# Two attention stages of a four-layer kernel: scores in row groups, a reordered step, and the residual moved to Pool

## The chip, the cores and the metric

One program runs on one core of a Trainium2 chip. The metric is the device time of one execution in microseconds; the kernel before took 2830.82 us (median of 3 runs, 2821.55 to 2833.54).

## The reference

Four layers act on x of shape 16 items x 256 tokens x 128 features. Each layer is: normalise, scale and shift (the "modulation"), attention, gated residual; then normalise, modulate, feed-forward, gated residual. The change touches the attention of layers 0 and 1 only.

```python
# layer 0 attention: 16 heads of 64
q = (x @ Wq).reshape(B, N, H, Dh)            # scale 64**-0.5
k, v = halves of x @ Wkv
s = einsum('bhid,bhjd->bhij', q * scale, k)
gm = max(s, axis=-1)                         # before masking
p = where(causal_mask, 0, exp(s - gm))
out = (p @ v) / (sum(p) + EPS)
return out.reshape(B, N, H * Dh) @ Wo + bo
# layer 1 attention: 8 heads of 128, plus scores of relative position, softmax, then @ w_out + b_out
# after either:  x = x + gate * attention(modulated(norm(x)))
```

## The kernel before, in words

Items are processed one after another. `walk` issues the same list of steps on each engine (PE, ACT, DVE, Pool, SP); an item has PER = 8 steps, there are 128 steps in a stage, and a loop body holds two items. Engines are coupled by semaphores only, so on each engine the order written in `step` is the order of execution. In a step `at`, `nx` (or `n1`, `n2`) are steps ahead whose projections are made, and `b1`, `b2`, `b3` are steps behind whose softmax, P^T and values are finished.

**Layer 0 (`attention0`, L393 to L633).** One step is one pair of heads. A = Wq Wk^T per head (64 rows deep, L496) is made once before the loop, for 16 heads, and split in a rounded and a rest part in fp32r. A product of two such split operands is `matmul3` (L120): three matmuls, recorded as L122, L123, L124. PE issues in a step: transposes of P for b2 (L383, six); scores of `at` as xA x hT, two heads one after the other, each 2 row blocks x 3 matmuls of 256 columns, 128 rows deep (L122 to L124, `xA` in the rows); projections xA for nx (two `matmul3`, with `A` in the rows) and between them V for nx in fp32 (L533); four small bf16 matmuls that add the causal mask (L540, L542), two for each head after its row maximum; P^T V for b2 in two column groups of 64 (L552); the output projection for b3 (L563). ACT copies o (L465), the second head's P^T (L469), rounds xA (L480, twice), copies V (L482) and makes the exponentials (L457, L459: two of each in a step). DVE copies the first head's P^T (L597), takes the row maxima (L602, one for each head), adds EPS, takes the reciprocal and scales P (L610, L612, L617), and writes the rest of xA (L625, twice). The residual of an item is on DVE: bias and gate at the end of the step with p = 2 (L183, L188), add and row statistics in the step p = 3 (L191, L195). Once per item, in step p = 5, PE transposes the normalised rows of the item after next (L507) into the free half of the bank of the first xA; ACT modulates and rounds them (L389, L131), Pool makes the rest (L138).

**Layer 1 (`attention1`, L925 to L1285).** One step is one head. PE: transposes of P (L1140), projection (A in the rows), scores (xA), in half of the steps the values (VO), six matmuls for the position scores (a_R), P^T V accumulated over the heads in one of two banks `y_ps` (L1190). SP writes the position scores to DRAM and reads them back shifted. ACT: P^T (L1051), xA (L1056), values (L1062), exponentials (L1074). DVE: L1246, L1249, L1253, the sum with the shifted scores and its maximum (L1265), L1270, position scores (L1276), and the residual as in layer 0. The item's transposes (L1179) go in step p = 3 into the free half of the bank `qh_ps` of the projection, so they wait for DVE's L1253, and the projection of step p = 4 waits for ACT's modulation (L389), which ACT does before the exponentials of that step.

Weights are loaded by DMA into an arena; in layer 0 the DVE waits for the gate's DMA before its loop.

Of the kernel before, what the change touches and what calls it, by code (L numbers as in the profile page):

```python
# [94 lines left out]
class Norms:  # L95


    def __init__(self, nc, ctx):
# [12 lines left out]
        self.delta = sb("delta", [P, NT, P])  # L111
        self.hT = sb("hT", [P, 2, T])
# [86 lines left out]
def residual_by_pool(pool, n, at, y, gate, y_ready, each, weighted, added, item=False):  # L199
# [4 lines left out]
    pool.tensor_tensor(n.delta[:], y, g, ALU.mult).then_inc(weighted, 1)  # L204
    wait(pool, weighted, at, item=True)
# [151 lines left out]
class Shared:  # L357
# [8 lines left out]
    [("wqT0", (16, P), 64), ("wkT0", (16, P), 64), ("wv0", (1024,), P), ("wo0", (8, P), P), ("bo0", (P,), P)],  # L366
# [26 lines left out]
def attention0(nc, d, k):  # L393
# [7 lines left out]
    with ExitStack() as ctx:  # L401
        def sb(name, shape):
            return ctx.enter_context(nc.sbuf_tensor("a0_" + name, shape, F32))

        A = ctx.enter_context(nc.sbuf_tensor("a0_A", [P, 2 * PER, 2, P], F32R))
        xA = ctx.enter_context(nc.sbuf_tensor("a0_xA", [P, 4, 2, T], F32R))
        v = sb("v", [P, 4, NT, P])
# [7 lines left out]
        xA_ps = k.banks[0:2]  # L415
        s_ps, pT_ps = k.banks[2:4], k.banks[4:6]
        o_ps, y_ps = k.banks[6], k.banks[7]
        names = ("chain", "var", "std", "rstd", "xn", "ht_mm", "ht", "ht_rounded", "ht_cut", "A_mm", "A_rounded", "A_cut",
                 "xA_mm", "xA_rounded", "xA", "v", "s_mm",
                 "nmax", "masked", "exp", "den", "rec", "p", "pT_mm", "pT0", "pT1", "o_mm", "oT", "y_mm", "res")  # L420
        s = signals(nc, ctx, "a0_", names)
        LAST, LEAD, LAG = PER - 1, 6, 4

        def halves(x, i, first, end):
            return [x[:, i, part, first:end] for part in range(2)]

        with nc.Block() as block:
# [5 lines left out]
            @block.gpsimd  # L433
            def _(pool):
                def step(at):
                    ni = at.shift(3)
                    if at.p == 5 and ni.real:
                        cut_hT_rest(pool, n, ni, s["ht_rounded"], s["ht_cut"])

                walk(pool, PER, 2, LEAD, LAG, step)  # L440

            @block.scalar
            def _(act):
                std_of_rows(act, n, s["var"], s["std"])
                for h in range(2 * PER):
                    act.wait_ge(s["A_mm"], h + 1)
                    act.activation(A[:, h, 0, :], k.banks[h % 4][:, 0:P], ACT.Identity, scale=64 ** -0.5
                                   ).then_inc(s["A_rounded"], 1)

                def step(at):  # L450
# [10 lines left out]

                    if b3.real:
# [7 lines left out]
                    if at.p == 5:  # L470
                        ni = at.shift(3)
                        if ni.real:
                            wait(act, s["ht_mm"], ni, item=True)
                            modulated(act, k, phase, ni, xA_ps[0][:, T:2 * T], n.hT[:, ni.s // PER % 2, :], s["ht"])
                            cut_hT(act, n, ni, s["ht"], s["ht_rounded"])
                    if nx.real:
                        wait(act, s["s_mm"], nx.shift(-2), 2)
                        for h in range(2):
                            wait(act, s["xA_mm"], nx, 2, 1 - h)
                            act.copy(xA[:, 2 * nx.ring(2) + h, 0, :], xA_ps[h][:, 0:T]).then_inc(s["xA_rounded"], 1)  # L480
                        wait(act, s["o_mm"], nx.shift(-4))
                        act.copy(v[:, nx.ring(4)], xA_ps[1][:, T:2 * T].rearrange("p (t d) -> p t d", t=NT)).then_inc(s["v"], 1)  # L482
# [8 lines left out]
            def _(pe):  # L491
                pe.wait_ge(k.weights_in[phase], 16 * weight_pieces(phase))
                for h in range(2 * PER):
                    if h >= 4:
                        pe.wait_ge(s["A_cut"], h - 3)
                    pe.matmul(k.banks[h % 4][:, 0:P], w["wqT0"][:, h, :], w["wkT0"][:, h, :], start=True, stop=True  # L496
                              ).then_inc(s["A_mm"], 1)
                pe.wait_ge(s["A_cut"], 2 * PER)

                def step(at):  # L500
                    nx, b1, b2, b3 = at.shift(1), at.shift(-1), at.shift(-2), at.shift(-3)
                    ni = at.shift(3)
                    if at.p == 5 and ni.real:
                        wait(pe, s["xn"], ni, item=True)
                        wait(pe, s["xA"], at, 2, 1)
                        for t in range(NT):
                            mm = pe.transpose(xA_ps[0][:, T + t * P:T + (t + 1) * P], n.xn[:, t, :], k.ident[:])  # L507
# [7 lines left out]
                    if at.real:  # L515
                        for h in range(2):
                            wait(pe, s["xA"], at, 2, 1 - h)
# [1983 lines left out]
```

## Time and profile before

| | |
|---|---|
| median of 3 runs | 2830.82 us |
| the profiled execution's own time | 2832.67 us |
| its span (first to last instruction) | 2831.0 us |
| busy PE, PEld, DVE, ACT, POOL over the span | 2580.4, 2224.2, 1999.8, 1420.3, 590.2 us |
| layer 0 attention, loop | about 46 to 697 us |
| layer 1 attention, loop | about 1020 to 1545 us |

PE is the tensor engine's matmuls, PEld its weight loads, which run beside them. A matmul's recorded duration holds its latency; what it costs in a stream is the distance from its start to the next one's. "x6" in a row of the timeline means six instructions of that kind in a row, told by the start of the first and the time to the end of the last.

### The profile page before, as it was taken

To read this page: it belongs to the slowest core of one execution; us is meant where nothing else is said; L and a number is where in the kernel's file an instruction comes from. 1 tells how busy PE (TensorE), PEld (TensorE's weight loads), DVE (VectorE), ACT (ScalarE), POOL (GpSimd) and SP (SyncE) were. 2 spreads that over 40 slices of the span, in tenths; PEclk is the share of its full clock that TensorE was granted. 3 is DMA by queue.
4 is the path that set the end of the run, shared out by engine and by line. 5 is a ranking of instruction groups with operands and counts; after the bars stand their busy time and mean duration, and the time that the engine had idled before them with its cause. 6 is when DMAs were issued, how large, how long until landed. Compare 5 with 4: busy or idle time off the path is not lost. (4 is left out here: it accounts for less than half of the span.)

```text
span 2831.0 us, 65632 instructions
## 1 busy us (share of the span) xinstructions
PE 2580.4 (91%) x21002; PEld 2224.2 (79%) x21064; DVE 1999.8 (71%) x6254; ACT 1420.3 (50%) x4003; POOL 590.2 (21%) x1099
## 2 busy tenths in 40 slices
PE   5999999998999999999997999968998886999898
PEld 5988888887888879999996999955665464666566
DVE  4888888887677658888887677756775325677687
ACT  3666666666555445566665322314555222455544
POOL 0000000000111100000000111136775025777322
PEclk9999999999999999999999999979999897999899
DMA  5000000001100145555554000037553753655100
GB/s 146 2 2 1 1 1 1 1 1 35 30 0 0 47 131 159 159 166 167 167 166 135 9 0 0 0 86 206 153 144 98 85 60 102 163 152 147 41 14 17
DMA packets 196040, 212.11 MB, mean 75 GB/s; under 512 B 12628, under 2 KB 179940, under 8 KB 194420
## 3 DMA queue, kind: packets, MB, share of 16 engines
q1 hardware_dynamic: 195828, 209.64, 27.8%
q8 instruction: 89, 1.46, 0.2%
q14 instruction: 123, 1.01, 0.1%
HBM read 108.95 MB, written 90.65 MB: 71 GB/s over the span
## 5 line engine op out<-in xcount | busy, mean ns | idle before, releaser
L138 POOL TENSOR_TENSOR hT<-hT 128x256 fp32r<-128x256 f32 x64 | 47.0, 735 | 1415.6 <-ACT hT L131 1415.6
L122 PE MATMUL bank<-hT,a_xA 128*128 128x256 f32 x768 | 228.0, 297 | 10.4 <-DVE a_top L1265 7.6
L123 PE MATMUL bank<-hT,a_xA 128*128 128x256 f32 x768 | 216.8, 282 | 0.0
L124 PE MATMUL bank<-hT,a_xA 128*128 128x256 f32 x768 | 216.3, 282 | 0.0
L602 DVE TENSOR_REDUCE a_nmax<-bank 128x2 f32<-128x512 f32 x256 | 175.0, 690 | 56.6 <-PE bank L124 54.3
L1074 ACT ACTIVATE a_p<-a_p,a_nmax 128x256 f32<-128x256 f32 x256 | 128.3, 502 | 163.5 <-DVE a_nmax L1270 163.5
L1723 ACT ACTIVATE a_p<-bank 128x1024 f32<-128x1024 f32 (+1 forms) x256 | 193.4, 808 | 24.2 <-PE bank L1778 20.0
L480 ACT CAST a_xA<-bank 128x256 fp32r<-128x256 f32 x256 | 95.0, 373 | 198.2 <-PE bank L124 198.2
L1351 ACT ACTIVATE f_silu<-bank 128x512 f32<-128x512 f32 x128 | 76.5, 598 | 214.9 <-PE bank L124 214.9
L799 ACT ACTIVATE f_hidden<-bank,arena 128x256 f32<-128x256 f32 x256 | 120.5, 473 | 114.9 <-PE bank L124 113.7
L862 PE MATMUL bank<-arena,f_hidden 128*128 128x128 f32 x1024 | 172.0, 288 | 6.4 <-DVE f_acc L916 5.0
L1666 POOL TENSOR_SCALAR_AFFINE_SELECT a_p<-a_p 128x512 f32<-128x512 f32 x256 | 163.8, 640 | 0.0
L916 DVE SCALAR_TENSOR_TENSOR f_acc<-bank,f_cw,f_acc 128x128 f32<-128x128 f32 x448 | 134.8, 345 | 40.0 <-PE bank L862 37.0
L1932 DVE TENSOR_REDUCE a_nmax<-bank 128x4 f32<-128x1024 f32 x128 | 155.6, 1216 | 3.9 <-PE bank L1765 3.9
L122 PE MATMUL bank<-hT,f_w 128*128 128x256 f32 x512 | 156.0, 305 | 0.3 <-POOL hT L138 0.3
L122 PEld LDWEIGHTS bank<-hT,a_xA 128*128 128x128 f32 x768 | 145.2, 189 | 13.0 <-issue 12.5
L862 PEld LDWEIGHTS bank<-arena,f_hidden 128*128 128x128 f32 x1024 | 137.0, 192 | 19.3 <-DVE f_acc L916 11.1
L123 PEld LDWEIGHTS bank<-hT,a_xA 128*128 128x128 f32 x768 | 145.5, 189 | 0.0
L123 PE MATMUL bank<-hT,f_w 128*128 128x256 f32 x512 | 145.5, 284 | 0.0
L124 PE MATMUL bank<-hT,f_w 128*128 128x256 f32 x512 | 145.4, 284 | 0.0
L124 PEld LDWEIGHTS bank<-hT,a_xA 128*128 128x128 f32 x768 | 145.2, 189 | 0.0
L1190 PE MATMUL bank<-a_v,a_pT 128*128 128x128 f32 x1024 | 136.3, 276 | 4.9 <-ACT a_pT L1051 4.9
(309 smaller groups left out, 8144.1 us busy)
## 6 DMA issues: line engine op xcount, KB each, us to landing
pos_dram<-a_pos SPq DMA_DIRECT2D x128, 383.0 KB
a_stack<-rows_dram SPq DMA_DIRECT2D x128, 320.0 KB, 4.1
rows_dram<-a_cut SPq DMA_DIRECT2D x192, 192.0 KB, 2.4
a_shifted<-pos_dram SPq DMA_DIRECT2D x128, 256.0 KB, 2.7
f_merged<-f_staged SPq DMA_DIRECT2D x16, 578.0 KB, 9.0
gate<-gates_dram SPq DMA_DIRECT2D x32, 256.0 KB, 10.8
arena<-in_task SPq DMA_DIRECT2D x4, 1156.0 KB, 8.4
x<-in_x SPq DMA_DIRECT2D x4, 512.0 KB, 8.3
```

Of the source, the lines that this page charges most:

```text
L122: pe.matmul(out, left[0], right[0], start=start, stop=False, skip_group_check=True)
L123: pe.matmul(out, left[0], right[1], start=False, stop=False, skip_group_check=True)
L124: return pe.matmul(out, left[1], right[0], start=False, stop=stop, skip_group_check=True)
L602: dve.tensor_reduce(nmax[:, at.ring(2), h, :], s_ps[h][:].rearrange("p (t k) -> p t k", t=NT), AX_X, ALU.max, negate=True).then_inc(s["nma ...
L799: act.activation(hidden[:, nx.ring(2), :], h_ps[nx.ring(2)][:, 0:T], ACT.Relu, bias=w["e1b"][:, nx.p:nx.p + 1]).then_inc(s["hidden"], 1)
L862: mm = pe.matmul(y, hidden[:, at.ring(2), t * P:(t + 1) * P], w["e2w"][:, at.p, :], start=(t == 0), stop=not last, skip_group_check=True)
L916: i = dve.scalar_tensor_tensor(out=a, in0=z, scalar=c[:, t, at.p:at.p + 1], in1=a, op0=ALU.mult, op1=ALU.add)
L1074: i = act.activation(p[:, at.ring(4), t, :], p[:, at.ring(4), t, :], ACT.Exp, bias=nmax[:, r, t:t + 1], accum_out=sums[:, r, t:t + 1])
L1190: mm = pe.matmul(y[:, t * P:(t + 1) * P], pT[:, b2.ring(2), j, t * P:(t + 1) * P], v[:, slot, j, h * P:(h + 1) * P], start=(b2.p == 0 and ...
L1666: pool.affine_select(blocks, blocks, [[0, 4], [1, P]], ALU.is_ge, 0.0, base=0, channel_multiplier=-1).then_inc(s["causal"], 1)
L1723: act.activation(p[:, b4.ring(2), first:end], sT_ps[:, first:end], ACT.Exp).then_inc(s["exp"], 1)
L1932: dve.tensor_reduce(nmax[:, half, 1, of], s_ps[:, 2 * T:6 * T].rearrange("p (c q) -> p c q", c=4), AX_X, ALU.max, negate=True).then_inc(s[ ...
```

## The change

In layer 0, A is no longer made: q and k are projected for both heads of a pair at once (`qk`, 128 rows = 2 heads x 64), and the scores are q^T k with 64 rows depth, head 0 on rows 0 to 63 of the array, head 1 on rows 64 to 127, issued alternately into two banks. V is projected in split fp32r, 256 columns wide (two head pairs) for one block of tokens per step. Both heads' scores signal once at their end. The mask of head 1 is issued after P^T V. In both layers the residual's bias, gate and add go to Pool, after ACT has copied the sum from PSUM (`take_sum`), and DVE keeps the statistics, one step later in layer 0. In layer 1 the item's transposes go into the free `y_ps` bank, and ACT does them after the exponentials. The copy of the first head's P^T by DVE is the same line before and after.

```diff
@@ helpers
+def take_sum(act, n, at, y, y_ready, biased, taken):
+    wait(act, y_ready, at)
+    wait(act, biased, at.shift(-at.per), item=True)
+    act.copy(n.y[:], y[:, 0:T].rearrange("p (t d) -> p t d", t=NT)).then_inc(taken, 1)
+
+def biased_residual_by_pool(pool, n, at, gate, bias, taken, biased, weighted, added):
+    wait(pool, added, at.shift(-at.per), item=True)
+    wait(pool, taken, at, item=True)
+    pool.tensor_tensor(n.delta[:], n.y[:], bias, ALU.add).then_inc(biased, 1)
+    wait(pool, biased, at, item=True)
+    g = gate[:, at.item, :].unsqueeze(1).to_broadcast([P, NT, P])
+    pool.tensor_tensor(n.delta[:], n.delta[:], g, ALU.mult).then_inc(weighted, 1)
+    wait(pool, weighted, at, item=True)
+    pool.tensor_tensor(n.x[:, at.item, :, :], n.x[:, at.item, :, :], n.delta[:], ALU.add).then_inc(added, 1)
@@ attention0, before the loop
-                for h in range(2 * PER):
-                    pe.matmul(k.banks[h % 4][:, 0:P], w["wqT0"][:, h, :], w["wkT0"][:, h, :], ...)
+                for i in range(6):        # ACT rounds, DVE makes the rest, 128x512 each
+                    act.activation(W[:, x, 0, part], whole, ACT.Identity, scale=scale).then_inc(s["W_rounded"], 1)
+                pool.wait_ge(k.gate_in[phase], 16 * GATE_PIECES)     # and no longer DVE
@@ attention0, PE
-                        for h in range(2):
-                            wait(pe, s["xA"], at, 2, 1 - h)
-                            wait(pe, s["exp"], at.shift(-1), 2, 1 - h)
-                            for t in range(NT):
-                                mm = matmul3(pe, s_ps[h][:, t * T:(t + 1) * T],
-                                             halves(xA, 2 * at.ring(2) + h, t * P, (t + 1) * P),
-                                             halves(n.hT2, at.s // PER % 2, 0, T), start=(t == 0))
-                            mm.then_inc(s["s_mm"], 1)
+                        wait(pe, s["qk"], at, 2)
+                        wait(pe, s["exp"], at.shift(-1), 2)
+                        for t in range(NT):
+                            for a, c in ((0, 0), (0, 1), (1, 0)):
+                                for h in range(2):
+                                    mm = pe.matmul(s_ps[h][:, t * T:(t + 1) * T],
+                                                   qk[64 * h:64 * h + 64, at.ring(2), 0, a, t * P:(t + 1) * P],
+                                                   qk[64 * h:64 * h + 64, at.ring(2), 1, c, :], ...)
+                        mm.then_inc(s["s_mm"], 1)
...
-                            for t in range(NT if h else 0):
-                                pe.matmul(xA_ps[1][:, T + t * P:T + (t + 1) * P], n.hT[:, item, t * P:(t + 1) * P],
-                                          w["wv0"][:, c:c + P], start=True, stop=True)
-                            matmul3(pe, xA_ps[h][:, 0:T], halves(A, 2 * nx.p + h, 0, P), halves(n.hT2, item, 0, T)
+                            if i:
+                                matmul3(pe, qk_ps[1][:, T:2 * T], halves(n.hT2, item, t * P, (t + 1) * P),
+                                        [W[:, 2, part, first:first + 2 * P] for part in range(2)])
+                            matmul3(pe, qk_ps[i][:, 0:T], [W[:, i, part, nx.p * P:(nx.p + 1) * P] ...
...
+                    if at.real:
+                        mask(0)
                     if b2.real:
                         ...               # P^T V
+                    if at.real:
+                        mask(1)
@@ attention1, PE
-                        if at.p == 4:
-                            wait(pe, s["ht"], at.shift(4), item=True)
...
-                        wait(pe, s["xA"], n2)
-                            mm = pe.transpose(qh_ps[:, T + t * P:T + (t + 1) * P], n.xn[:, t, :], k.ident[:])
+                        wait(pe, s["taken"], ni.shift(-2 * PER), item=True)
+                            mm = pe.transpose(y_ps[ni.s // PER % 2][:, t * P:(t + 1) * P], n.xn[:, t, :], k.ident[:])
```

## Rows read from the trace of the kernel before

**Rows 1.** The page, part 1: busy us, share and instructions of each engine.

```profile
PE 2580.4 (91%) x21002; PEld 2224.2 (79%) x21064; DVE 1999.8 (71%) x6254; ACT 1420.3 (50%) x4003; POOL 590.2 (21%) x1099
```

**Rows 2.** Busy time by window: PE, PEld, DVE, ACT, POOL (count), then clock, DMA.

```profile
50.00:690.00 640.00, 633.03 (x5603) 567.65 (x5602) 519.60 (x1502) 436.10 (x1686) 11.00 (x15) 1.00 0.01 2
1020.00:1545.00 525.00, 501.11 (x3675) 482.26 (x3673) 428.54 (x1643) 306.23 (x863) 11.11 (x15) 0.99 0.51 160
```

**Rows 3.** Source view of L480: count, min/median/max ns, first and last start.

```profile
L480 ACT CAST a_xA<-bank x256: 372/373/378, 47.3 to 684.6; 128x256 fp32r<-128x256 f32 x128
```

**Rows 4.** Timeline of PE, one step of layer 0: start, us, instruction, count.

```profile
300.84 0.37 PE L122 MATMUL bank<-hT,a_xA 128*128 128x256 f32 x1
...
302.35 0.28 PE L122 MATMUL bank<-hT,a_A 128*128 128x256 f32 x1
...
302.70 0.61 PE L533 MATMUL bank<-arena,hT 128*128 128x128 f32 x4
303.06 0.36 PE L122 MATMUL bank<-hT,a_A 128*128 128x256 f32 x1
...
303.51 0.23 PE L540 MATMUL bank<-causal_bf,ident_bf 128*128 128x128 bf16 x1
...
303.69 0.22 PE L542 MATMUL bank<-causal_bf,ident_bf 128*128 128x128 bf16 x1
303.83 0.87 PE L552 MATMUL bank<-a_pT,a_v 128*64 128x256 f32 x8
304.64 0.71 PE L563 MATMUL bank<-arena,a_oT 128*128 128x128 f32 x4
305.18 0.82 PE L383 MATMUL bank<-ident,a_p 128*128 128x128 f32 x6
305.76 0.36 PE L122 MATMUL bank<-hT,a_xA 128*128 128x256 f32 x1
...
311.02 0.36 PE L122 MATMUL bank<-hT,a_xA 128*128 128x256 f32 x1
```

**Rows 5.** Timeline of PE in windows of 70 and 90 ns inside L552.

```profile
303.83 0.44 PE L552 MATMUL bank<-a_pT,a_v 128*64 128x256 f32 x2
...
304.43 0.28 PE L552 MATMUL bank<-a_pT,a_v 128*64 128x128 f32 x2
```

**Rows 6.** Timeline of ACT, same step.

```profile
303.70 0.37 ACT L480 CAST a_xA<-bank 128x256 fp32r<-128x256 f32 x1 [0.43 <-PE bank L124]
...
305.74 0.23 ACT L459 ACTIVATION_READ_ACCUMULATOR a_p<-bank,a_nmax 128x1 f32 x1
```

**Rows 7.** Timeline of DVE, same step.

```profile
301.83 1.41 DVE L602 TENSOR_REDUCE a_nmax<-bank 128x2 f32<-128x512 f32 x2 [0.48 <-PE bank L124]
...
304.49 0.75 DVE L625 TENSOR_TENSOR a_xA<-bank,a_xA 128x256 fp32r<-128x256 f32 x2
```

**Rows 8.** Timeline of all engines, first item of layer 0.

```profile
42.92 0.60 DVE L171 TENSOR_SCALAR xn<-x,row_mean,row_rstd 128x128 f32<-128x128 f32 x2 [3.29 <-DMA gate<-gates_dram]
...
45.45 0.72 POOL L138 TENSOR_TENSOR hT<-hT 128x256 fp32r<-128x256 f32 x1 [44.93 <-ACT hT L131]
...
46.23 0.58 PE L122 MATMUL bank<-hT,a_A 128*128 128x256 f32 x1 [1.90 <-POOL hT L138]
```

**Rows 9.** Timeline of DVE, end of layer 0.

```profile
696.99 0.42 DVE L183 TENSOR_TENSOR delta<-bank,arena 128x256 f32<-128x256 f32 x1 [2.43 <-PE bank L563]
...
698.37 0.49 DVE L195 BATCH_NORM_STATS2 row_stats<-x 128x6 f32<-128x128 f32 x2
```

**Rows 10.** Source view of L206, Pool's add in other stages.

```profile
L206 POOL TENSOR_TENSOR x<-x,delta x64: 722/732/995, 731.6 to 2826.8; 128x256 f32<-128x256 f32 x32, 128x256 f32 x32
```

**Rows 11.** Timeline of layer 1, PE around the item's transposes.

```profile
1299.02 0.34 PE L124 MATMUL bank<-a_R,hT 128*128 128x384 f32 x1
1299.95 0.44 PE L1179 MATMUL bank<-ident,xn 128*128 128x128 f32 x2 [0.59 <-DVE a_xA L1253]
```

**Rows 12.** Waits in 1050 to 1540 us: us in total, times, longest.

```profile
PE bank L1179 <- DVE a_xA L1253: 10.0, 14, 1.3
```

More of the change, by code:

```diff
@@ L492, in _ @@
                 pe.wait_ge(k.weights_in[phase], 16 * weight_pieces(phase))
[L493 to L498, printed above, removed]
+                pe.wait_ge(s["W_cut"], 6)
                 def step(at):
@@ L556, in step @@
                         mm.then_inc(s["o_mm"], 1)
+                    if at.real:
+                        mask(1)
                     if b3.real:
                         wait(pe, s["oT"], b3)
-                        before = b3.shift(-PER)
-                        if b3.p == 0 and before.real:
-                            pe.wait_ge(s["chain"], before.item * 3 + 3)
+                        if b3.p == 0:
+                            wait(pe, s["taken"], b3.shift(-PER), item=True)
                         for t in range(NT):
@@ L604, in step @@
                                               negate=True).then_inc(s["nmax"], 1)
-                    if after:
-                        residual(at.shift(-4), "stats").then_inc(s["res"], 1)
+                    if at.p == 4 and at.shift(-5).real:
+                        row_stats(dve, n, at.shift(-5), s["added"])
                     if b1.real:
@@ L1184, in step @@
                         y, slot, h = y_ps[b2.s // PER % 2], b2.s // 4 % 2, b2.p % 4
-                        before = b2.shift(-2 * PER)
-                        if b2.p == 0 and before.real:
-                            pe.wait_ge(s["chain"], before.item * 3 + 3)
+                        if b2.p == 0:
+                            wait(pe, s["ht"], b2, item=True)
                         for t in range(NT):
@@ L1226, in _ @@
                 dve.wait_ge(s["r_in"], 16)
-                dve.wait_ge(k.gate_in[phase], 16 * GATE_PIECES)
-                def residual(item, *parts):
-                    y = y_ps[item.s // PER % 2]
-                    return add_residual(dve, n, item, y[:, 0:T].rearrange("p (t d) -> p t d", t=NT),
-                                        k.gate[phase % 2], w["bo1"].unsqueeze(1).to_broadcast([P, NT, P]), s["chain"],
-                                        3, parts)
                 def step(at):
                     n2, b1, b3 = at.shift(2), at.shift(-1), at.shift(-3)
-                    ended = b3.real and b3.p == LAST
-                    after = at.shift(-4).real and at.p == 3
-                    if after:
-                        residual(at.shift(-4), "add")
                     if at.p == 1 and at.shift(7).real:
@@ L1255, in step @@
                                                  op0=ALU.add, op1=ALU.subtract).then_inc(s["xA"], 1)
-                    if after:
-                        residual(at.shift(-4), "stats").then_inc(s["res"], 1)
+                    if at.p == 3 and at.shift(-4).real:
+                        row_stats(dve, n, at.shift(-4), s["added"])
                     if at.real:
@@ L1278, in step @@
                         i.then_inc(s["pos"], 1)
-                    if ended:
-                        wait(dve, s["y_mm"], b3)
-                        residual(b3, "bias")
-                    if ended:
-                        residual(b3, "gate")
                 walk(dve, PER, 2, LEAD, LAG, step)
```

142 lines of the change are left out of this document (76 added, 66 removed).

## The prediction

> **What bounds the kernel now.** Start with the page: PE is busy for 91% of the span, but that is a mean over eight stages [rows 1]. The windows give the two stages that are edited: in layer 0's loop PE is busy 633 of 640 us, DVE 520, ACT 436; in layer 1's loop PE 501 of 525 and DVE 429 [rows 2]. Both are PE's. The source view gives layer 0's step: 256 roundings are 128 steps, the first at 47.3 and the last at 684.6, about 0.8 us of which lies inside a step, so 636.5 / 127 = 5.01 us each, 40.1 us an item [rows 3]. The timeline shows a plain step, from the first score at 300.84 to the next at 305.76: 4.92 us without a hole, and then one of 5.26 [rows 4]. Matmuls of 256 columns start 0.118 us apart: three go from 302.35 to 302.70.
>
> The parts of the plain step, start to start [rows 4]: 12 scores 1.42 (1.51 as recorded, the first takes over 0.09 from the transposes); the two projections 0.71; V 0.44 (0.36 and the 0.09 of late start that follows); masks 0.23; a gap of 0.09; P^T V from 303.83 to 304.64, 0.81; output projection 0.54; six transposes 0.66. Sum 4.90.
>
> **Layer 0, PE.** Whether scores of 64 rows run in pairs no row shows. The nearest is P^T V, in two column groups: both starts of a pair fall in one window of 70 ns, twice [rows 5]. Its eight records take 0.81 us; four fp32 records of 128 columns alone need 0.11 each, and four of 256 at least twice that, 1.3 us one after another. So column groups run in pairs, their weight loads too. I take the same for row groups: 6 pairs x 0.118 = 0.71 instead of 1.42. The other end is no overlap at all, 12 x 0.118 = 1.42. I choose the first, since the partner of each matmul is in another bank and other rows, as it is in other columns there.
>
> A change of shape is not free in the same rows: between the end of the last mask (303.69 + 0.06) and L552 are 0.09 us, and L552's last records start at 304.43 and stream 0.11, but L563 begins at 304.64, another 0.09, and its first weights are then loaded with nothing beside them, 0.11 [rows 4, 5]. So scores cost 0.71 + 0.09 + 0.11 = 0.91 and the projections behind them 0.20 more.
>
> The Trainium skill (TensorEngine Tiling (Array Packing), Key Properties) says that tiles load and multiply in parallel and that a change of tiling mode drains the engine; by this rule the sum is the one just made. Against it stands the skill's TensorE: Matmul & The Clock Gate, section LDWEIGHTS: a load is priced by its columns, not its rows, so a 64-row load is no cheaper than a full one. Were the twelve loads to queue on one port, they alone would fill what was saved. The column rows here halve the columns of each load and can't decide that.
>
> New PE sum: scores 0.91; projections q, k and V now nine matmuls of 256 columns, 1.06 + 0.20; masks 0.23; P^T V with its gap 0.90; output projection 0.54; transposes 0.66. That is 4.50, 0.42 less.
>
> **Layer 0, what is late next.** The scores of the next step must now wait for both heads' exponentials; before, head 1's could lag by half of the scores. Follow ACT: its second rounding begins at 303.70, 0.20 after the last projection matmul has streamed (303.51), and it works without a hole until 305.97, the last accumulator read: 2.27 us [rows 6]. New cycle: first loads 0.11, scores 0.71, switch and projections 1.26, 0.20 to ACT, 2.27, 0.04 back to PE: **4.59 us**. The masks fit beside it: head 1's mask ends about 1.3 us after the projections, and ACT, with two copies and head 0's exponentials in front of it (over half of the 2.27), gets there 1.5 us after them. Follow DVE: from L602 at 301.83 to the end of the second L625 (304.49 + 0.75) 3.41 us [rows 7]; cycle 0.11 + 0.71 + 0.20 + 3.41 + 0.04 = 4.47. The three chains lie within 0.12 of each other; I take ACT's, 4.59, 0.33 less than before.
>
> Once per item: before, the 5.26 step (DVE's add and statistics hold up L625) and 0.22 for two transposes make 0.57 [rows 4]. After: the statistics alone (0.49, rows 9) on a DVE with 0.12 to spare, +0.35; the item's transposes wait for the first rest of q, ready about 0.4 after PE comes by, and are 0.22 themselves, of which 0.18 lies in PE's slack, +0.43; the projections wait for the modulation, which ACT can't start before it has done the exponentials and two copies, +0.4. Together 1.2, 0.6 more than now. The loop's own branch stays (40.1 against 8 x 4.92 + 0.57 = 39.9). Item: 40.1 - 8 x 0.33 + 0.6 = 38.1. **16 x -2.0 = -32 us.** The ends of this term: PE's sum alone, 4.50 with no extras, -54 - 10 = about -62; no overlap, below.
>
> Row maximum, EPS, scaling, P^T copies: unchanged, nothing. That DVE evicts the first head's P^T, as the change is described, is so before it too: 0.
>
> **Ends of layer 0.** Before the loop 16 products, roundings and rests go, six roundings and rests of 128x512 come, on ACT and DVE side by side. What starts the loop is the gate's DMA, on which DVE waits before L171 at 42.92, and PE begins at 46.23 [rows 8]. Afterwards only Pool waits for it; xn, modulation and rounding can be done before, and Pool's 0.72 follows at once: 42.9 + 0.8 = 43.7, **-2.5 us** (0 if the six pieces take until 43). At the end DVE's bias, gate and add take 696.99 to 698.37, 1.38 us [rows 9]; ACT's copy of 256 columns (0.37 by L480) and three Pool operations of 0.74 [rows 10] make 2.6 to 2.7: **+1.3 us**. The same at the end of layer 1, **+1.3**. Inside the loop Pool has one other task per item, two steps later, and 2.3 us against a step of 4.6 hide; without that cover the hT rest would be late by what sticks out.
>
> **Layer 1.** At the item's transposes PE's stream ends at 1299.02 + 0.17, and L1179 starts at 1299.95, since DVE's L1253 in the same bank is late behind the residual [rows 11]; 14 such waits are listed, 10.0 us by the modelled ends [rows 12], 0.76 us each by the starts, 16 x 0.76 = 12. Both causes go: other bank, no residual on DVE. Late next is ACT, where the modulation with its rounding now stands behind the exponentials and before the next P^T copy and L1056; DVE may then wait for L1056. I take 2 us off: **-10 us**; ends 0 (all given back) and -20 (DVE's 1.4 us an item also shorten other waits).
>
> **Sum.** -32 - 2.5 + 1.3 + 1.3 - 10 = -42. Against the profiled execution's own 2832.67 us: 2790.8; the median of the runs lies 1.9 lower. I say **2790**.
>
> **Rivals.**
> (1) *No pairs: row groups run, or load, one after another.* For it: a load of 128 columns can't start in the neighbour's shadow if there is one port, and 12 loads at 0.11 are the old 1.42 again. Against: the pairs of L552 [rows 5]. It decides from about 0.18 us a pair upwards. Scores 1.42 + 0.20; ACT's cycle 4.59 + 0.71 = 5.30, 0.38 over now: 128 x 0.38 = +49, extras +10, the rest -10: **2880**, slower. Chance 12%.
> (2) *Half pairs*, 0.18 a pair: ACT's cycle 4.59 + 0.37 = 4.96, +5, +10, -10: **2835**. 8%.
> (3) *The three chains trip each other.* 4.47, 4.50 and 4.59 with single buffers give more than their maximum; at 4.75 a step: 128 x -0.17 = -22, extras +10, rest -10: **2811**. For it: DVE already has waits of both kinds; against: most are on PE. 18%.
> (4) *Switching is hidden* (the 0.09s are waits of semaphores and loads overlap): cycle 4.59 - 0.31 = 4.28, bound 4.3 by DVE's too: -80, extras 0, rest -10: **2745**; halfway 2765. 12%.
> That the layer 1 part does nothing is +10 on any of them.
>
> **Numbers.** Forecast 50%, 2770 to 2805 for itself. Range **2755 to 2845**: it leaves out rival 1 and the far half of rival 4. About 0.5% (14 us) is what a measurement of this kernel tells from no change: faster than 2817 are the forecast, (4) and most of (3), 78%; within, the rest of (3) and half of (2), 9%; slower 13%.
>
> **What would show it.** Scores: twelve 64-row records from first to last start in about 0.6 us, pairs under 10 ns apart; in rival 1 equal distances of 0.12. First score to next first score 4.6; before the scores PE waits on L457/L459's line by about 0.1. The L1179 wait gone, an item of layer 1 shorter by 0.6. PE's first projection at 43.7. Tails 1.3 longer. The forecast is wrong if the scores' part is over 1.2 us, or if ACT's run from the last projection to the last exponential is not 2.3.

## The result, and the profile after

The kernel after takes 2811.77 us (median of 7 runs, 2806.77 to 2814.26) against 2830.82: ratio 0.9933, 95% interval 0.9921 to 0.9944. That is 19 us faster where 40 were forecast; the profiled span went from 2831.0 to 2806.8. The direction was right and about half of the size was missing.

The page's first part and the windows of the two edited loops, in the columns of [rows 1, 2]:

```profile
PE 2535.8 (90%) x20904; PEld 2129.8 (76%) x20904; DVE 1971.7 (70%) x6148; ACT 1416.5 (50%) x4025; POOL 660.1 (24%) x1195
```

```profile
50.00:680.00 630.00, 594.18 (x5506) 482.47 (x5504) 496.71 (x1463) 442.37 (x1707) 45.74 (x63) 1.00 0.01 2
1030.00:1500.00 470.00, 464.07 (x3415) 446.29 (x3414) 395.26 (x1482) 277.04 (x817) 44.59 (x59) 1.00 0.53 166
```

PE was busy in 99% of layer 0's loop and is now busy in 94%: it waits. Layer 1's is still PE's. The source view that answers to [rows 3] has the first rounding at 44.0 and the last at 665.2, where before had 47.3 and 684.6:

```profile
L513 ACT CAST a_qk<-bank x256: 372/372/405, 44.0 to 665.2; 128x256 fp32r<-128x256 f32 x128
```

A plain step on PE, in the timeline that answers to [rows 4]:

```profile
318.25 0.98 PE L549 MATMUL bank<-a_qk 64*128 64x256 f32 x12 [0.25 <-ACT a_p L490]
319.15 0.38 PE L123 MATMUL bank<-hT,a_W 128*128 128x256 f32 x1
...
320.20 0.28 PE L125 MATMUL bank<-hT,a_W 128*128 128x256 f32 x1
320.32 0.23 PE L571 MATMUL bank<-causal_bf,ident_bf 128*128 128x128 bf16 x1
...
320.54 0.87 PE L586 MATMUL bank<-a_pT,a_v 128*64 128x256 f32 x8
...
321.96 0.85 PE L403 MATMUL bank<-ident,a_p 128*128 128x128 f32 x6
322.92 0.98 PE L549 MATMUL bank<-a_qk 64*128 64x256 f32 x12
```

and on ACT, as in [rows 6]:

```profile
320.51 0.37 ACT L513 CAST a_qk<-bank 128x256 fp32r<-128x256 f32 x1 [0.33 <-PE bank L125]
320.78 0.38 ACT L515 COPY a_v<-bank 128x256 f32<-128x256 f32 x1
...
322.55 0.23 ACT L490 ACTIVATION_READ_ACCUMULATOR a_p<-bank,a_nmax 128x1 f32 x1
```

Twelve 64-row scores take 0.90 us to the next matmul's start, where they took 1.42: they run in pairs. From the first to the last start they need 0.70 us. The step is 4.67 instead of 4.92, and it is ACT's circle: PE's last projection has streamed at 320.32, ACT starts 0.19 later, works until 322.78, and PE's next scores start 0.14 after that.

Once an item in layer 0, Pool's three residual operations meet DVE. DVE and then Pool in the step from 298.15, which is 4.97 long:

```profile
299.17 1.29 DVE L628 TENSOR_REDUCE a_nmax<-bank 128x2 f32<-128x512 f32 x2 [0.86 <-PE bank L549]
300.37 0.63 DVE L636 TENSOR_SCALAR a_den<-a_sums 128x4 f32<-128x4 f32 x1
301.04 0.18 DVE L638 RECIPROCAL a_rec<-a_den 128x4 f32<-128x4 f32 x1
```

```profile
299.33 0.73 POOL L224 TENSOR_TENSOR delta<-delta,gate 128x256 f32<-128x256 f32 x1 [0.19 <-POOL delta L221]
300.25 0.73 POOL L226 TENSOR_TENSOR x<-x,delta 128x256 f32 x1 [0.19 <-POOL delta L224]
```

An operation on 4 elements a row that otherwise takes 0.16 us lasts 0.63 and ends when Pool's does. The reduces beside Pool's L224 keep their time. What DVE loses reaches PE, whose transposes wait for the scaled P (L643):

```profile
302.32 0.88 PE L403 MATMUL bank<-ident,a_p 128*128 128x128 f32 x6 [0.28 <-DVE a_p L643]
```

In the next step the statistics come in front of L636, and PE stands before the item's transposes:

```profile
305.35 0.47 DVE L233 BATCH_NORM_STATS2 row_stats<-x  x2
```

```profile
307.53 0.44 PE L535 MATMUL bank<-ident,xn 128*128 128x128 f32 x2 [0.53 <-DVE a_qk L651]
```

The start of layer 0, all engines, as [rows 8], and the end of it, as [rows 9]:

```profile
42.13 0.72 POOL L139 TENSOR_TENSOR hT<-hT 128x256 fp32r<-128x256 f32 x1 [41.61 <-DMA gate<-gates_dram]
...
42.91 0.58 PE L123 MATMUL bank<-hT,a_W 128*128 128x256 f32 x1 [4.49 <-POOL hT L139]
...
57.36 0.41 PE L124 MATMUL bank<-hT,a_W 128*128 128x256 f32 x1
...
61.58 0.28 PE L124 MATMUL bank<-hT,a_W 128*128 128x256 f32 x1
...
677.63 0.37 ACT L214 COPY y<-bank 128x256 f32<-128x256 f32 x1 [0.80 <-PE bank L598]
678.14 0.72 POOL L221 TENSOR_TENSOR delta<-y,arena 128x256 f32<-128x256 f32 x1 [26.93 <-ACT y L214]
...
679.74 0.72 POOL L226 TENSOR_TENSOR x<-x,delta 128x256 f32<-128x256 f32 x1
680.50 0.49 DVE L233 BATCH_NORM_STATS2 row_stats<-x 128x6 f32<-128x128 f32 x2 [5.30 <-POOL x L226]
```

### The profile page after: what moved, and what is told of

The parts are those of the page before. It is cut to its first block and busy times, and to the rows that moved or that the text cites. A ratio compares the mean times of both kernels' runs of the same rounds, so it can differ in the third digit from the quotient of the medians.

```text
span 2806.8 us, 65268 instructions
## 1 busy us (share of the span) xinstructions
PE 2535.8 (90%) x20904; PEld 2129.8 (76%) x20904; DVE 1971.7 (70%) x6148; ACT 1416.5 (50%) x4025; POOL 660.1 (24%) x1195
## 5 line engine op out<-in xcount | busy, mean ns | idle before, releaser
L628 DVE TENSOR_REDUCE a_nmax<-bank 128x2 f32<-128x512 f32 x256 | 164.9, 686 | 98.9 <-PE bank L549 98.9
L221 POOL TENSOR_TENSOR delta<-y,arena 128x256 f32<-128x256 f32 x32 | 24.7, 772 | 787.9 <-ACT y L214 787.9
L513 ACT CAST a_qk<-bank 128x256 fp32r<-128x256 f32 x256 | 95.0, 374 | 163.3 <-PE bank L125 163.3
L883 PE MATMUL bank<-arena,f_hidden 128*128 128x128 f32 x1024 | 171.6, 288 | 6.4 <-DVE f_acc L937 5.2
L549 PE MATMUL bank<-a_qk 64*128 64x256 f32 x1536 | 126.2, 295 | 15.7 <-ACT a_p L490 5.4
L1217 PEld LDWEIGHTS bank<-a_v,a_pT 128*128 128x128 f32 x1024 | 131.7, 193 | 6.6 <-ACT a_pT L1081 5.4
L1417 PE MATMUL bank<-arena,f_hidden 128*128 128x128 f32 x1024 | 136.0, 276 | 0.0
L549 PEld LDWEIGHTS bank<-a_qk 64*128 64x128 f32 x1536 | 102.5, 187 | 40.7 <-DVE a_qk L651 27.4
L1292 DVE TENSOR_TENSOR a_pos<-bank,arena 128x384 f32<-128x384 f32 x256 | 130.7, 551 | 2.7 <-PE bank L125 2.4
```

The lines of the kernel that those rows point to most:

```text
L549: mm = pe.matmul(s_ps[h][:, t * T:(t + 1) * T], qk[64 * h:64 * h + 64, at.ring(2), 0, a, t * P:(t + 1) * P], qk[64 * h:64 * h + 64, at.rin ...
L628: dve.tensor_reduce(nmax[:, at.ring(2), h, :], s_ps[h][:].rearrange("p (t k) -> p t k", t=NT), AX_X, ALU.max, negate=True).then_inc(s["nma ...
L883: mm = pe.matmul(y, hidden[:, at.ring(2), t * P:(t + 1) * P], w["e2w"][:, at.p, :], start=(t == 0), stop=not last, skip_group_check=True)
L1217: mm = pe.matmul(y[:, t * P:(t + 1) * P], pT[:, b2.ring(2), j, t * P:(t + 1) * P], v[:, slot, j, h * P:(h + 1) * P], start=(b2.p == 0 and ...
L1417: mm = pe.matmul(y_ps[at.ring(2)][:, t * P:(t + 1) * P], hidden[:, at.ring(2), c * T + t * P:c * T + (t + 1) * P], w["w3"][:, at.p, c, :], ...
```

## The experiments

Step and item lengths are read start to start, each from one trace. The first four columns of them are medians over the loop of layer 0: the plain step, step 3 to 4 (from the first score of p = 3 to that of p = 4, where Pool's residual runs), step 4 to 5 (statistics and the item's transposes), and an item. The last column is the mean of items 6 to 14 of layer 1. Steps of layer 1 are read by the transposes of P and counted in the texts from the one with the item's transposes (p = 3), so its third step is that of p = 5 and its last that of p = 2. Ratio and interval are those to the kernel before as measured beside each kernel; its median was 2828.7 us beside e1 to e4, 2829.46 beside e5 to e8, 2830.61 beside e9 to e11 and 2826.88 beside e12. The ratio is not the quotient of the two medians and differs from it by up to 0.0016 (e12: 0.9802).

```
kernel                   median us  ratio  interval          plain  3-4   4-5   item 0  item 1
before                   2830.82    1                        4.91   5.26  5.13  39.90   31.34
after                    2811.77    0.9933 [0.9921, 0.9944]  4.68   4.91  5.44  38.62   31.04
e1_layer1_only           2828.77    0.9997 [0.9987, 1.0008]  4.91   5.26  5.13  39.90   31.02
e2_pool_narrow           2802.05    0.9914 [0.9896, 0.9932]  4.68   4.68  5.43  38.43   30.70
e3_no_eps                2802.54    0.9907 [0.9888, 0.9925]  4.68   4.68  5.23  38.25   31.01
e4_heads_in_turn         2844.39    1.0058 [1.0041, 1.0074]  5.00   5.00  5.75  40.84   31.04
e5_tr_and_stats_late     2803.61    0.9911 [0.9886, 0.9937]  4.69   4.91  4.72  37.77   30.98
e6_layer1_residual_dve   2819.37    0.9973 [0.9957, 0.9989]  4.69   4.91  5.44  38.63   31.57
e7_gate_late             2810.52    0.9935 [0.9910, 0.9961]  4.69   4.91  5.44  38.64   30.95
e8_v_late                2799.14    0.9897 [0.9871, 0.9924]  4.53   4.77  5.44  37.69   31.03
e9_late_all              2791.16    0.9861 [0.9846, 0.9876]  4.53   4.77  4.72  37.02   31.00
e10_modulation_later     2782.36    0.9826 [0.9813, 0.9840]  4.53   4.77  4.72  37.04   30.69
e11_reduces              2785.57    0.9830 [0.9817, 0.9844]  4.53   4.76  4.71  37.02   30.66
e12_apart                2771.02    0.9818 [0.9804, 0.9832]  4.53   4.51  4.71  36.74   30.53
```

**Which layer gave it.** `attention0` and its weights are those of before.

> The changed layer 1 with layer 0 as before. My theory, from the two traces: layer 1 brings 5.0 us inside its loop and its tail costs 1.6, so the kernel is 3 to 4 us faster than before (ratio 0.9985 to 0.999), and the other 16 us are layer 0's. Rival, my prediction's own term (-10 + 1.3): 9 us faster, ratio 0.997.

2828.77 us, no measurable gain; by the interval it is at most 4 us, so that all or nearly all of the 19 us are layer 0's. An item in the middle of layer 1 is 0.3 us shorter and the loop 4 us, from 510.1 to 506.1 (first to last step, by the transposes of P), but its end costs 1.5 more, and the first items (35.1, 31.9, 33.0, 36.7 us in this trace; 34.4, 31.7, 33.1, 36.0 before) give nothing.

**Pool and DVE: is it the meeting?** Pool's three operations keep their places and waits.

```diff
-    pool.tensor_tensor(n.delta[:], n.y[:], bias, ALU.add)
+    pool.tensor_tensor(n.delta[:, :, 0:1], n.y[:, :, 0:1], bias[:, :, 0:1], ALU.add)
```

> The changed kernel, with Pool's three residual operations on one column of 128 in both attentions (the residual of the other 127 columns is left out). Theory A: DVE's tensor_scalar with both operands in SBUF stands still while a Pool operation runs (L636 up to 0.65 us against 0.16, L1265 up to 0.84 against 0.35, L1286 up to 0.60 against 0.17; 6.1 us in layer 0 and 12.6 us in layer 1 together). Then no such instruction is longer than its median by over 0.2 us, the step p=3 of layer 0 goes from 4.91 to 4.68, the item of layer 1 from 31.0 to 30.3, and the kernel is 8 to 16 us faster than the changed one (2796 to 2804). Rival B: DVE has slack there and the layer 1 item is held by the round trip of the positions through DRAM; then the long instructions go but the time moves by less than 3 us.

It is. The source view of L636 here, and of L1265 and L1286 in the kernel after (count, min/median/max ns):

```profile
L636 DVE TENSOR_SCALAR a_den<-a_sums x128: 151/160/163, 57.5 to 669.9; 128x4 f32<-128x4 f32 x128
```

```profile
L636 DVE TENSOR_SCALAR a_den<-a_sums x128: 151/160/652, 57.0 to 672.3; 128x4 f32<-128x4 f32 x128
...
L1265 DVE TENSOR_SCALAR a_p<-a_p,a_rec x256: 345/353/839, 1012.1 to 1516.3; 128x256 f32<-128x256 f32 x128
...
L1286 DVE TENSOR_SCALAR a_nmax<-a_top x128: 168/170/596, 1010.3 to 1514.5; 128x2 f32<-128x2 f32 x128
```

Step 3 to 4 falls to 4.68, the length of a plain step, and layer 1's item to 30.70: there the third step was 3.72, where 3.44 is what PE needs. The rows show this clearly; the medians less so, since the interval overlaps that of the kernel after.

**Does DVE's chain bound the plain step?** The addition of EPS is left out, 0.16 us and a wait.

```diff
-    dve.tensor_scalar(den[:, r], sums[:, r], EPS, None, ALU.add).then_inc(s["den"], 1)
-    wait(dve, s["den"], b1)
-    dve.reciprocal(rec[:, r], den[:, r]).then_inc(s["rec"], 1)
+    dve.reciprocal(rec[:, r], sums[:, r]).then_inc(s["rec"], 1)
```

> The changed kernel without the addition of EPS in layer 0's softmax (DVE L636 and the wait behind it left out, 0.2 us of each step). Theory A: the plain step of 4.68 us is DVE's chain (both maxima, EPS, reciprocal, four scalings, two rests, then the next scores), so it falls by 0.1 to 0.2, down to ACT's or PE's own 4.5 to 4.59: 12 to 23 us faster than the changed kernel. Rival B, the prediction's chain: ACT holds the step; then the step stays at 4.6 to 4.68 and the time moves by less than 3 us.

The plain step doesn't move (4.68), so DVE isn't on it. Steps 3 to 4 and 4 to 5 fall by 0.2 each: in those DVE is on it, once through the stop and once through the statistics. With 0.23 and 0.21 in 15 items, these two are worth 6.6 us, and the median is about 7 under that of the kernel after: less than theory A and more than theory B forecast.

**Are the pairs the gain?** The same twelve matmuls, head 0's six first.

```diff
-    for t in range(NT):
-        for a, c in ((0, 0), (0, 1), (1, 0)):
-            for h in range(2):
+    for h in range(2):
+        for t in range(NT):
+            for a, c in ((0, 0), (0, 1), (1, 0)):
```

> The changed kernel with the twelve score matmuls issued head by head (six on rows 0 to 63, then six on rows 64 to 127) instead of alternately; nothing else. Theory A: only neighbours in different row groups run together, so the scores take 12 x 0.118 less one pair, about 1.3 us instead of 0.7, and with the chains full the step becomes 5.3: 128 x 0.6 = 75 us slower than the changed kernel, 2887. Rival B: the engine looks further ahead and overlaps the groups whatever the order: within 10 us of the changed kernel.

The kernel is slower than before. Its scores, in PE's timeline:

```profile
307.74 1.29 PE L549 MATMUL bank<-a_qk 64*128 64x256 f32 x12
308.96 0.39 PE L123 MATMUL bank<-hT,a_W 128*128 128x256 f32 x1
```

1.22 to the next line's start instead of 0.90, and a step of 5.00, the same 0.32 more. Neither theory's number came: one after another they would take 12 x 0.118 + 0.20 = 1.6. From the first to the last start are 1.01 us (0.70 in the kernel after), and three times in this step two starts lie 5 to 9 ns apart, so matmuls of the two row groups still ran beside each other. In which order the engine took them the records don't settle.

**The step of 5.44.** The statistics go behind L651 on DVE, the item's transposes behind those of P on PE; nothing else.

> The changed kernel; in layer 0 PE makes the item's transposes after those of P instead of before, and DVE takes the row statistics after the rests of q and k. Theory A: the 5.63 us step (0.95 over the plain one) is the statistics (0.4) on DVE's chain in front of the rests and PE idle for the rest of q (0.53) with 0.66 us of P transposes queued behind; both go, the item falls by 0.6 to 0.9, 16 items: 10 to 14 us faster than the changed kernel. Rival B: ACT's modulation is late by as much, since it waits for the item's transposes, and PE's projections wait for it: under 4 us.

Step 4 to 5 falls to 4.72 and the item by 0.85. In this trace, which is of the fastest of the four executions, 12 us of the layer 0 loop are gone (621.2 to 609.1, first to last score); of the ratio to before 0.0022, 6 us, with intervals that overlap. Both moves were made at once, so their shares are not told apart.

**Layer 1's residual back on DVE**, with the new place of the transposes kept:

```diff
-                    if at.p == 2 and at.shift(-3).real:
-                        biased_residual_by_pool(pool, n, at.shift(-3), ...)
+                    if ended:
+                        wait(dve, s["y_mm"], b3)
+                        residual(b3, "bias")
+                        residual(b3, "gate")
```

> The changed kernel with layer 1's residual back on DVE (bias, gate, add); the item's transposes stay in the y bank and behind no wait. Theory A: the 0.75 us wait at the item's transposes went with the bank, not with the residual; DVE pays 1.3 us an item but is no longer stopped by Pool (0.84 an item), and the tail is 1.6 shorter: within 4 us of the changed kernel. Rival B: DVE's chain in layer 1 is full, the item grows by 0.5 to 1.3: 8 to 20 us slower.

Its ratio is 0.0040 over that of the kernel after, 11 us slower. In its trace the step with the item's transposes is as short as in the kernel after (4.36), but the next one takes 4.64 for 4.14. So in layer 1 DVE hasn't the 1.4 us an item to give: Pool's part avoids a loss there, and its own costs (the stops, the longer end) are smaller than that.

**The head.** Pool waits for the gate only before its first residual.

```diff
-                pool.wait_ge(k.gate_in[phase], 16 * GATE_PIECES)
...
                     if at.p == 3 and at.shift(-4).real:
+                        pool.wait_ge(k.gate_in[phase], 16 * GATE_PIECES)
```

> The changed kernel, in layer 0 Pool waits for the gate's DMA only before the first residual. Theory A: PE's first projection starts at about 40.2 instead of 42.9 us, because Pool's first rest of hT (42.13) waited for the gate alone, and the stretch at the lower clock shrinks with the pause: 3 to 5 us faster. Rival B: PE starts earlier and spends the same number of steps at the lower clock: 2.7 us faster.

The first step's scores start at 44.2 instead of 46.4, and the first item remains at 42.8 us (score to score), so the 2.2 us are still there when the second item begins, nearer to theory B's 2.7 than to theory A's 3 to 5. Of them 1.4 are left at the last step's scores (666.2 instead of 667.6). The median tells no difference, and its interval is too wide for one of 2 us.

**ACT's chain.** V's copy leaves the place between roundings and exponentials. DVE's second rest no longer waits for it, and PE's next V does.

```diff
-                        act.copy(v[:, nx.s // 2 % 4, nx.p % 2, :], qk_ps[1][:, T:2 * T]).then_inc(s["v"], 1)
                     if at.real:
                         exps(0)
                     if at.real:
                         exps(1)
+                    if nx.real:
+                        ...
+                        act.copy(v[:, nx.s // 2 % 4, nx.p % 2, :], qk_ps[1][:, T:2 * T]).then_inc(s["v"], 1)
```

> The changed kernel; in layer 0 ACT copies V (0.27 us start to start) after the exponentials of the step, not before, and DVE's rest of k no longer waits for it; PE's next V waits for the copy. Theory A: the plain step of 4.68 is ACT's chain: 0.20 + 2.27 from the last projection to the last exponential, and 0.15 from there to PE's next scores where I had put 0.04; 0.27 out of it brings the step to PE's or DVE's own 4.5 to 4.56: 15 to 23 us faster than the changed kernel. Rival B: DVE's chain is as long (4.47 with the same 0.1 more for the hand-back is 4.57 to 4.68): the step stays above 4.6, under 8 us.

The plain step falls to 4.53 (scores from 314.83 to 319.36), near the PE sum of 4.50 in the prediction. That ACT's chain was the bound is shown: 0.27 taken out of it shortens the step by 0.15, where e3 had taken 0.2 out of DVE's without effect. It shortens it by no more than 0.15 because another circle is then as long. Head 1's exponentials now start 0.31 after the start of that head's last mask matmul, the same in one plain step after the other, so they wait for it; in the kernel after the distance was 0.44 and ACT came late by itself. PE's scores still start 0.14 after ACT's last read:

```profile
317.99 0.22 PE L576 MATMUL bank<-causal_bf,ident_bf 128*128 128x128 bf16 x1
```

```profile
318.30 0.37 ACT L488 ACTIVATE a_p<-bank,a_nmax 128x128 f32<-128x128 f32 x1
...
319.02 0.20 ACT L490 ACTIVATION_READ_ACCUMULATOR a_p<-bank,a_nmax 128x1 f32 x1
```

PE issues that mask behind P^T V. Whether an earlier mask would bring the step below 4.53 no run tried.

**All three together.**

> The three moves together: V's copy behind the exponentials, the item's transposes behind those of P, the row statistics at the end of DVE's step, and Pool's wait for the gate only before the first residual. Theory A (each takes a piece of its own off ACT's or DVE's chain, the pieces add): plain steps 4.53 us as in the kernel with V late, the step with the lock 4.76, the next two 4.57 and 4.61 (4.72 and 4.76 less 0.15), so 36.6 an item for 38.6: 16 x -2.0 = -32, 2780 us. Theory B (PE's own 4.50 a step is now the wall: what is taken off one chain is mostly the other's slack): the steps with more work on PE (two transposes, 0.22) stay at 4.75, an item 37.2, -22, 2790.

2791.16 us. Item 37.02, near theory B: step 4 to 5 carries PE's additional 0.22 and is 4.72. Step 5 to 6 is 4.78 for another reason: its first projection starts 1.16 after the scores instead of 0.90, since ACT's modulation (L409) is late.

```profile
335.44 0.38 PE L123 MATMUL bank<-hT,a_W 128*128 128x256 f32 x1 [0.18 <-ACT hT L409]
```

**Layer 1's modulation one step later**, behind the rounding of xA.

```diff
-                    if at.p == 3:
-                        ni = at.shift(5)
+                    if at.p == 4:
+                        ni = at.shift(4)
```

> As e9_late_all, and layer 1's modulation with its rounding one step later, behind the rounding of the next head's xA, so that it stands in nobody's way. Theory A (the 0.28 us lost in the third step of each item of layer 1 is ACT's, held by the modulation): that step 3.72 -> 3.44, 15 x -0.28 = -4 us against e9. Theory B (it is DVE's stop beside Pool's operations alone, as the kernel with the narrow Pool operations says): no difference to e9, 0 +- 1 us, and the step stays at 3.72.

The third step falls to 3.44 (theory A), although the stops of DVE remain (L1286's longest is 592 ns). The 0.28 needed both delays, DVE's stop and the modulation in front of xA, and either removed is enough (e2 and here). The median is 9 us lower where the steady items explain 4; the first items vary by as much between traces, and the rest stays open.

**Another kind of operation on DVE.**

```diff
-    dve.tensor_scalar(den[:, r], sums[:, r], EPS, None, ALU.add)
+    dve.tensor_reduce(den[:, r], sums[:, r], AX_X, ALU.add)
...
-    dve.tensor_scalar(nmax[:, r], top[:, r], -1.0, None, ALU.mult)
+    dve.tensor_reduce(nmax[:, r], top[:, r].unsqueeze(2), AX_X, ALU.max, negate=True)
```

(sums has a second column that holds EPS.)

> As e9_late_all, and two of DVE's SBUF to SBUF tensor_scalars become tensor_reduces of the same result: layer 0's sum + EPS (a reduce over the sum and a stored EPS) and layer 1's negation of the row maximum. Theory A (only the operation's kind makes DVE stand still beside Pool, and the trace shows no reduce that does): layer 0's fourth step 4.76 -> 4.53, 15 x -0.23 = -3.5 us, and of layer 1's 12.6 us of stopped DVE time the 5.4 of the negation go, the third step 3.72 -> 3.5: -3; in all 6 us under e9. Theory B (any DVE operation that reads and writes SBUF beside Pool stops; the reduces were spared because they read PSUM): maxima of about 0.65 us for the new reduces, and no gain, 0 +- 2 us against e9.

Theory A is right for layer 1: the third step is 3.44. The new reduce (L1288) starts 13 times inside a Pool operation with up to 0.56 us of it still to come, and is never longer than 157 ns:

```profile
L1288 DVE TENSOR_REDUCE a_nmax<-a_top x128: 154/155/157, 988.9 to 1489.7; 128x2 f32<-128x2 f32 x128
```

In layer 0 the step stays at 4.76, and the reduce there tests nothing: in e9 the addition of EPS in its place had no stop any more (longest 167 ns). The tensor_scalar behind it, the scaling of P, is stopped. Source view:

```profile
L646 DVE TENSOR_SCALAR a_p<-a_p,a_rec x512: 272/341/637, 54.4 to 651.6; 128x128 f32<-128x128 f32 x86, 128x256 f32<-128x256 f32 x85
```

The same line as L644 had 635 in e9: once V is late, the meeting is there anyway.

**Kept apart.** On top of e10, in both layers, with the negation as a reduce:

```diff
+                        wait(pool, s["p"], at.shift(-1))
                         biased_residual_by_pool(pool, n, ...)
```

> As e10_modulation_later, and Pool kept apart from DVE's SBUF to SBUF tensor_scalars: in both layers Pool's residual waits until DVE has scaled the P of that step, so that its three operations (2.2 us) fall where DVE reads PSUM; layer 1's negation of the maximum, which would still meet them, becomes a reduce. Theory A (DVE stops only where a tensor_scalar and a Pool operation meet, and which one it meets is a matter of placing; in e11 the stop had moved from the EPS add, now a reduce, to the scaling of 128x128, 637 ns for 285): no tensor_scalar over 1.1 times its median in either loop, layer 0's fourth step 4.77 -> 4.53, 15 x -0.24 = -3.6 us, layer 1 nothing more than e10 has (its items are at 30.7): 2778. Theory B (a Pool operation that starts 3 us later makes the statistics or the next rest of hT late, or the fourth step's 0.24 is ACT's additional copy of y, not DVE's stop): the step stays at 4.77 or another one grows, 2782 or more.

Theory A by the rows, and the lowest median: 2771.02 us against 2826.88, ratio 0.9818 [0.9804, 0.9832]. The scaling of P in both layers, and Pool's first operation, which now starts behind it:

```profile
L645 DVE TENSOR_SCALAR a_p<-a_p,a_rec x512: 277/316/350, 54.6 to 647.5; 128x128 f32<-128x128 f32 x86, 128x256 f32<-128x256 f32 x85
...
L1267 DVE TENSOR_SCALAR a_p<-a_p,a_rec x256: 344/352/358, 985.3 to 1473.1; 128x256 f32<-128x256 f32 x128
```

```profile
290.79 0.73 POOL L221 TENSOR_TENSOR delta<-y,arena 128x256 f32<-128x256 f32 x1 [31.44 <-DVE a_p L645]
```

No scaling of P is over its usual time, and step 3 to 4 is 4.51. In layer 1's trace every item from the fourth to the fourteenth is 30.5 long, and the last step of an item is 3.44 where e10 has 3.57. The interval lies below that of e9; with those of e10 and e11 it overlaps, and by the ratios e12 gains 2 us on e10.

## Why the prediction came out as it did

The mechanism came as forecast, pairs on PE and then a bound by ACT. Three terms of the sum failed: the hand-over from ACT back to PE (0.04 us put down, 0.14 measured, in each of 128 steps), Pool's residual priced as hidden although it stops DVE (0.23 us an item in layer 0), and the 2 us taken off in layer 1 for what is late next (7 to 8 measured, and a longer end).

**The bound.** PE's, as read from [rows 2]; after it ACT's, as forecast. Right.

**PE's step.** 6 pairs of 0.118, a switch and exposed loads: 0.82 for loads and scores and 1.26 for the projections make 2.08, and measured are 320.32 - 318.25 = 2.07. The sum of 4.50 was never alone on the path; the plain steps of e8 and later, 4.51 to 4.53, are just over it. With the rule of the Trainium skill that was weighed there (TensorEngine Tiling (Array Packing), Key Properties), that tiles load and multiply in parallel, the trace agrees: 0.90 us for twelve. Rival 1, one port for the loads, and rival 2, half pairs, are out. Taking the column groups of [rows 5] as the model for row groups was what decided this, and it was right.

**ACT's step.** 2.27 and 0.20 were 2.27 and 0.19. The term that failed is the last one, "0.04 back to PE": it is 0.14. The 0.04 had no row behind it. The hand-over PE to ACT had one, 0.20, and the way back should have been priced like it. The step came out 0.09 longer than forecast (4.68 for 4.59), 128 x 0.09 = 11.5 us, the largest part of what is missing. It brought the step to 4.68, towards rival 3's 4.75, and the time to its 2811, but not for its reason: e3 takes 0.2 off DVE's chain and the plain step stays, so the chains don't trip each other; one of them is simply longer.

**Once per item.** 1.2 forecast; 4.91 + 5.44 + 4.88 - 3 x 4.68 = 1.19 measured. The sum hides that a term is missing and others were too large: 0.23 is DVE's stop beside Pool (e2), which the prediction excluded by pricing Pool's work as hidden behind a step of 4.6; it asked whether Pool has time, not whether DVE has it meanwhile. The trace of the kernel before had the stop already. Its addition of EPS, beside Pool's one operation of an item (L138), took 0.20 to 0.33 us in each of 15 items instead of 0.16:

```profile
L610 DVE TENSOR_SCALAR a_den<-a_sums x128: 149/160/333, 58.1 to 691.7; 128x4 f32<-128x4 f32 x128
```

The item was forecast 2.0 shorter, 40.1 to 38.1. The mean over 14 items, without the first and the last, went from 40.2 to 39.0, and from the second item's start to the last rounding the loop lost 18.6 us, 1.24 for each of 15 items: 15 x 0.76 = 11 us short, the same 11.5 seen from the other side.

**The head.** PE's first projection came at 42.91 for 43.7 forecast, 3.3 us earlier. But the first item takes 42.1 us instead of 39.6 (by its roundings). PE stood for 4.5 us before the loop and then for 1.2 and 3.4 us before scores of the first steps (before: 1.9 and 2.8), and its 256-column matmuls keep to 0.41 us until 57.6, the 1.2 GHz level, where before they had 0.28 (2.4 GHz) from 51.3 on. Of 3.3 us, 0.8 are left. That the lower level comes from the pauses is not shown. In e7 PE starts another 2.2 us earlier and stands 2.0 instead of 4.5 before the loop; the later pauses (1.2 and 3.4) and the first item are the same as here, and the 2.2 are kept up to the second item.

**The ends.** 1.3 each forecast. Copy to statistics is 677.63 to 680.50, 2.87, where [rows 9] has 1.38: +1.5; for layer 1, from the last y to the next stage's first transpose, 10.8 to 12.5, +1.6. Right, a little low: Pool's operations start 0.80 apart, not 0.74.

**Layer 1.** -10 forecast, nothing measured (e1). The wait of [rows 12] is gone in full: the step that had it went from 5.19 to 4.36, 0.83 for the forecast 0.76. The 2 us off for what is late next should have been 7 to 8 (12 - 15 x 0.30): 0.28 in the third step, by DVE's stop together with the modulation that ACT has in front of xA (e2, e10, e11 each remove it), and 0.26 in the last (3.44 to 3.70), which is 3.47 in e11 and gone in e12, and whose cause no run isolates. The end takes 1.6 more, and what is left, 3 us, is as much as the first items differ from trace to trace.

**The sum** in spans: layer 0's items -18.6, its head -0.8, its end +1.5; layer 1 -5.4 in the loop and +1.6; together -21.7 of -24.2, the rest in stages that nobody edited. The layer 1 part is one profiled execution's; e1's runs give it as zero, and then -18 is left, near the medians' -19.

The Trainium skill (SBUF — State Buffer, Who interferes with whom) says that DVE and GpSimd share a pair of ports that the first to issue holds for the whole instruction, that tensor_scalar can take it, and that on trn2 tensor_reduce never does. Row and rule agree here: up to 652 ns for 160 at the tensor_scalar L636, and at most 157 for e11's reduce L1288 beside the same Pool operations. The other order shows too: Pool's L221 in layer 1 begins while DVE's L1265 runs, in each of 15 items, and takes 0.78 to 0.86 us for 0.73. The prediction left the page out, and it was the rule that spoke against this change. Its price as measured is step 3 to 4's 0.23 x 15 and the third step of layer 1's 0.28 x 15, together 7.7 us, and e2 came out 0.0019 of 2829, 5 us, under after, with intervals that overlap.

## What to carry to other kernels

Where several engines pass a step round in a circle, price every hand-over, in both directions, by a row; at 128 steps a hundredth of a microsecond is more than one. Work given to Pool is not free because Pool is idle: look at which tensor_scalars on DVE run at that time, and let Pool's operations start behind them. Compare the longest record of a line with its median in the trace that you have; here 333 ns for 160 stood in it before the change. When a bound moves from PE to ACT, look in ACT's queue for what stands between a wait and its consumer and needn't; here it was V's copy, worth 0.15 us of every step.

## What the runs showed of the hardware

- 64-row fp32r matmuls of 256 columns in different row groups and banks, queued alternately, run in pairs, a pair every 0.118 us, with their weight loads. Of steps 21 to 120, 26 have all six pairs 3 to 4 ns apart; in the others most pairs start about 32 ns apart (step of 318.25: first pair 3, the rest 31 to 34). The twelve need 0.70 us from first to last start either way. Queued group by group, not alternately, twelve of them still took 1.22 us to the next matmul instead of 0.90, less than one after another.
- A DVE tensor_scalar of fp32 from SBUF to SBUF that starts inside a Pool operation (tensor_tensor of 128x256 fp32) stands still until it ends, at 2, 4, 128 and 256 elements a row alike (596, 652, 637 and 839 ns for 170, 160, 285 and 353). Reduces (at most 157 ns for 155), the reciprocal of 4 elements (179 for 178) and whatever reads PSUM kept their times.
- From the end of ACT's last accumulator read to PE's waiting matmul 0.14 us; from a PE matmul's last column (its start plus 0.12) to ACT's copy 0.19; from one Pool operation to the next that waits for it 0.19 in the loop and 0.08 at its end.
